# Flamingo block: transposed FFN tile in the down projection's bank, centred residual on ScalarE, quantisation factors on GpSimd, one addition of maxima divided over VectorE and ScalarE

## What is computed

```python
def _bitlinear(x, w):
    return jnp.einsum('bsi,oi->bso', _act_quant(x), _weight_quant(w))
# _act_quant: scale = 127 / max|x| per row; round(x * scale) / scale
# _weight_quant: scale = 1 / mean|w|; clip(round(w * scale), -1, 1) / scale

x = x + tanh(g_xattn) * attention(layernorm(x), ctx, ctx)      # softmax(q k / 4 + causal) v, then Wo
y = layernorm(x)
x = x + tanh(g_ffn) * bitlinear(silu(bitlinear(y, w_gate)) * bitlinear(y, w_up), w_down)
```

## Time and profile before

| | |
|---|---|
| median of 3 runs | 1917.84 us (1916.58 to 1918.06) |
| profiled execution | 1916.38 us |
| its span, first to last instruction | 1914.7 us |
| PE busy | 1618.2 us, 85% |
| DVE busy | 1568.8 us, 82% |
| ACT busy | 1193.0 us, 62% |
| POOL busy | 1130.4 us, 59% |
| mean granted TensorE clock | 0.986 of full speed |

### The profile page before, as it was taken

How to read it: one execution, slowest core, us unless ns; L and a number is a source line. 1 busy time by engine, 2 the same in 40 slices (tenths; PEclk the granted TensorE clock), 3 DMA queues, 4 the chain that set the end, 5 groups by cost and what they waited for, 6 DMA issues and landing times.

```text
span 1914.7 us, 45148 instructions
## 1 busy us (share of the span) xinstructions
PE 1618.2 (85%) x15430; PEld 1306.4 (68%) x15430; DVE 1568.8 (82%) x3481; ACT 1193.0 (62%) x2505; POOL 1130.4 (59%) x1745
## 2 busy tenths in 40 slices
PE   3688888888888888888888888888888888888874
PEld 2667767777776776777777776677677777677752
DVE  4388888888888888888888888888888888888884
ACT  2366666666666666666666666666666666666652
POOL 4556666656666566566665666656656666566621
PEclk9899999999999999999999999999999999999997
DMA  3322222222222322322222222232232222222200
GB/s 107 106 82 96 76 85 90 83 87 81 96 74 81 100 75 78 98 76 84 92 80 90 81 94 76 81 100 76 78 98 75 86 90 76 92 84 91 74 26 11
DMA packets 116595, 158.25 MB, mean 83 GB/s; under 512 B 14609, under 2 KB 66961, under 8 KB 116369
## 3 DMA queue, kind: packets, MB, share of 16 engines
q1 hardware_dynamic: 115088, 155.24, 24.6%
q10 hardware_dynamic: 1280, 0.14, 0.1%
HBM read 37.88 MB, written 16.78 MB: 29 GB/s over the span
## 4 chain that ended last, share of the span: by engine, by line
PE 48%; DVE 16%; issue 15%; ACT 15%; POOL 2%; POOLq 0%; ACTq 0%; DVEq 0%
PE psum L574 12%; PE psum L493 7%; PE psum L590 7%; ACT h_t L714 6%; PE psum L483 6%; PE psum L516 5%; PE psum L559 5%; DVE h L795 4%; DVE gu L791 4%; ACT prob_t L684 3%; PE psum L468 3%; DVE st L810 3%; DVE x L807 3%; PE psum L475 3%; ACT o_raw L720 2%
## 5 line engine op out<-in xcount | busy, mean ns | idle before, releaser
L768 DVE TENSOR_REDUCE row_max<-psum 128x8 f32<-128x1024 f32 x256 | 311.0, 1215 | 20.0 <-PE psum L475 19.5
L677 ACT ACTIVATE s_low<-psum,row_max 128x128 f32<-128x128 f32 x1024 | 279.6, 397 | 16.6 <-DVE row_max L768 16.5
L684 ACT ACTIVATE prob_t<-psum 128x1024 f32<-128x1024 f32 x256 | 262.3, 1025 | 32.0 <-PE psum L483 27.8
L483 PE MATMUL psum<-ident,s_low 128*128 128x128 f32 x2048 | 266.6, 274 | 0.2
L483 PEld LDWEIGHTS psum<-ident,s_low 128*128 128x128 f32 x2048 | 236.2, 142 | 24.9 <-DVE s_low L775 0.6
L971 POOL TENSOR_SCALAR hq<-h,sm 128x1024 f16<-128x1024 f32 x128 | 142.9, 1116 | 181.6 <-DVE sm L847 181.6
L791 DVE SCALAR_TENSOR_TENSOR gu<-th,psum 128x512 f32<-128x512 f32 x256 | 174.8, 683 | 84.3 <-ACT th L692 83.9
L692 ACT ACTIVATE th<-psum,sm 128x512 f32<-128x512 f32 x256 | 184.4, 720 | 80.5 <-PE psum L574 80.5
L951 POOL TENSOR_SCALAR xc<-x,ln 128x256 f32<-128x256 f32 x128 | 61.3, 479 | 282.9 <-DVE ln L816 282.9
L574 PE MATMUL psum<-wg_t,xq_t 128*128 128x512 f16 x512 | 154.9, 384 | 70.3 <-DVE h L795 70.3
L475 PE MATMUL psum<-k_stk,q_stk 128*128 128x256 f32 x1024 | 211.0, 328 | 0.0
(11 more groups left out here) (112 smaller groups left out, 3607.6 us busy)
## 6 DMA issues: line engine op xcount, KB each, us to landing
k_stk<-k_t SPq DMA_DIRECT2D x384, 128.0 KB, 2.3
q_stk<-q_t SPq DMA_DIRECT2D x192, 256.0 KB, 2.5
c_in<-in_ctx SPq DMA_DIRECT2D x64, 256.0 KB
x_in<-in_x SPq DMA_DIRECT2D x64, 256.0 KB
out<-y SPq DMA_DIRECT2D x128, 128.0 KB
g_nat<-in_L_ffn_w_gate SPq DMA_DIRECT2D x1, 1024.0 KB, 8.3
g_nat<-in_L_ffn_w_up SPq DMA_DIRECT2D x1, 1024.0 KB, 10.7
g_nat<-in_L_ffn_w_down SPq DMA_DIRECT2D x1, 1024.0 KB, 12.6
```

The lines of the kernel that those rows point to most:

```text
L483: last = nc.tensor.transpose(S_B[half][:, n * P:(n + 1) * P], s_low[:, HPC * half + n, :], ident[:, :])
L677: last = nc.scalar.activation(s_low[:, HPC + n, :], S_B[1][:, n * P:(n + 1) * P], ACT.Identity, bias=row_max[:, HPC + n:HPC + n + 1])
L684: nc.scalar.activation(prob_t[:, HPC * half:HPC * (half + 1), :].rearrange("p h k -> p (h k)"), S_B[half], ACT.Exp).then_inc(p_ok[half], 1)
L768: nc.vector.tensor_reduce(out=row_max[:, HPC * half:HPC * (half + 1)], in_=S_B[half].rearrange("p (h k) -> p h k", k=P), axis=AX.X, op=ALU ...
```

## The change

Six things are changed.

1. `T16`, into which `hidden_t` transposes hq, moves from bank 5 to bank 7. PE's `gate_up(0)` no longer waits for h_t of its section but for h of the section before; `hidden_t` takes over the waits for y, the residual and v_sb that `down` had.
2. xc is made by ACT (`centre`): x1 times -1 plus the mean. Its sign is the opposite of before, and the rounded gate and up matrices are made with a minus sign at set-up. The negated mean on DVE (L815) and xc on POOL (L951) go.
3. The factors L831 and L847 are made by POOL, ahead of the quantisation that uses them.
4. The addition of maxima for half 0 is divided: DVE does heads 0 to 3 with one instruction of 128x512, ACT does heads 4 to 7 with four of 128x128 (`shift_first`).
5. The order in the bodies of PE, DVE, ACT and POOL is another, and on ACT it differs between even and odd sections.
6. `values` comes with half 0 first.

```diff
-        T16 = bank(5).bitcast(F16)
+        T16 = bank(7).bitcast(F16)
...
                 def gate_up(c, half):
                     if half == 0:
                         pe.wait_ge(xqt_ok, c.tile(2))
-                        wait(pe, ht_ok, c.tile(3))
+                        wait(pe, h_ok[1], c.tile(3))
...
                 def hidden_t(c):
+                    wait(pe, y_ok, c.tile(4))
+                    pe.wait_ge(x1_ok, min(c.tile(2), N_SEQ))
+                    if c.s == 0 and c.spreads:
+                        pe.wait_ge(v_ok, c.even + 4)
                     pe.wait_ge(hq_ok, c.tile(3))
...
                 def shifted_t(c, half):
                     pe.wait_ge(s_sub[half], c.tile(0))
+                    if half == 0:
+                        pe.wait_ge(s_sub_act, c.tile(0))
...
+                def shift_first(c):
+                    act.wait_ge(s_max[0], c.tile(0))
+                    wait(act, p_tr[0], c.tile(1))
+                    for n in range(HPC // 2, HPC):
+                        last = nc.scalar.activation(s_low[:, n, :], S_B[0][:, n * P:(n + 1) * P], ACT.Identity,
+                                                    bias=row_max[:, n:n + 1])
+                    last.then_inc(s_sub_act, 1)
...
+                def centre(c):
+                    act.wait_ge(ln2_ag, c.tile(1))
+                    wait(act, xq_ok, c.tile(2))
+                    nc.scalar.activation(xc[:, :], x1[:, 1 - c.s, :], ACT.Identity, bias=mv2[:, 0:1], scale=-1.0).then_inc(xc_ok, 1)
...
-                    nc.vector.tensor_tensor(s_low[:, 0:HPC, :], S_B[0].rearrange("p (h k) -> p h k", k=P),
-                                            row_max[:, 0:HPC].unsqueeze(2).to_broadcast((P, HPC, P)), ALU.add).then_inc(s_sub[0], 1)
+                    few = HPC // 2
+                    nc.vector.tensor_tensor(s_low[:, 0:few, :], S_B[0][:, 0:few * P].rearrange("p (h k) -> p h k", k=P),
+                                            row_max[:, 0:few].unsqueeze(2).to_broadcast((P, few, P)), ALU.add).then_inc(s_sub[0], 1)
...
-                    nc.vector.tensor_scalar(ln2[:, 0:1], mv2[:, 0:1], -1.0, None, ALU.mult)
...
-                    dve.wait_ge(x_rcp_ok, c.tile(1))
-                    nc.vector.tensor_scalar(row(sm, t, X_FACTOR), row(sm, t, X_RCP), ln2[:, 2:3], QMAX,
-                                            ALU.mult, ALU.mult).then_inc(x_factor_ok, 1)
...
-                    dve.wait_ge(h_rcp_ok, c.tile(2))
-                    nc.vector.tensor_scalar(row(sm, t, H_FACTOR), row(sm, t, H_RCP), row(sm, t, H_OWN), QMAX,
-                                            ALU.mult, ALU.mult).then_inc(h_factor_ok, 1)
...
-                    nc.gpsimd.tensor_scalar(xc[:, :], x1[:, t, :], ln2[:, 0:1], 1.0, ALU.add, ALU.mult).then_inc(xc_ok, 1)
...
                 def quantise(c):
+                    pool.wait_ge(x_rcp_ok, c.tile(1))
+                    nc.gpsimd.tensor_scalar(row(sm, t, X_FACTOR), row(sm, t, X_RCP), ln2[:, 2:3], QMAX,
+                                            ALU.mult, ALU.mult).then_inc(x_factor_ok, 1)
...
                 def quantise_hidden(c):
+                    pool.wait_ge(h_rcp_ok, c.tile(2))
+                    nc.gpsimd.tensor_scalar(row(sm, c.s, H_FACTOR), row(sm, c.s, H_RCP), row(sm, c.s, H_OWN), QMAX,
+                                            ALU.mult, ALU.mult).then_inc(h_factor_ok, 1)
```

More of the change, by code:

```diff
@@ L184, in _ @@
                     act.wait_ge(g_rnd, n + 1)
-                    nc.scalar.activation(g_tern[:, n, :], g_nat[:, n, :], ACT.Copy, bias=-ROUND32).then_inc(tern, 1)
+                    sign = -1.0 if n < 2 else 1.0
+                    nc.scalar.activation(g_tern[:, n, :], g_nat[:, n, :], ACT.Copy, bias=-sign * ROUND32, scale=sign).then_inc(tern, 1)
             @block.gpsimd
@@ L630, in body @@
                         if c.attn:
+                            values(c, 0)
                             values(c, 1)
-                            values(c, 0)
                     else:
@@ L641, in body @@
                             inputs_t(c)
+                        if c.outp:
+                            out_natural(c)
+                        if c.ffn:
+                            gate_up(c, 0)
                         if c.down:
@@ L733, in body @@
                 def body(c):
[L734 to L755, removed]
-                    if c.attn:
-                        values(c)
+                    if c.s == 0:
+                        if c.ffn:
+                            quant_t(c)
+                        if c.attn:
+                            shift_first(c)
+                        if c.projects:
+                            inputs_t(c)
+                        if c.down:
+                            hidden_t(c)
+                        if c.outp:
+                            out_t(c)
+                        if c.ffn:
+                            tanh(c, 0)
+                        if c.attn:
+                            shift(c)
+                            exp(c, 0)
+                        if c.outp:
+                            centre(c)
+                        if c.ffn:
+                            tanh(c, 1)
+                        if c.projects:
+                            project_qk(c)
+                        if c.attn:
+                            exp(c, 1)
+                            values(c)
+                    else:
+                        if c.ffn:
+                            quant_t(c)
+                        if c.projects:
+                            inputs_t(c)
+                        if c.attn:
+                            shift_first(c)
+                        if c.ffn:
+                            tanh(c, 0)
+                        if c.down:
+                            hidden_t(c)
+                        if c.outp:
+                            out_t(c)
+                        if c.attn:
+                            shift(c)
+                        if c.ffn:
+                            tanh(c, 1)
+                        if c.attn:
+                            exp(c, 0)
+                        if c.projects:
+                            project_qk(c)
+                        if c.outp:
+                            centre(c)
+                        if c.attn:
+                            exp(c, 1)
+                        if c.projects:
+                            project_v(c)
+                        if c.attn:
+                            values(c)
@@ L767, in top @@
                     wait(dve, s_sub[half], c.tile(1))
+                    if half == 0:
+                        wait(dve, s_sub_act, c.tile(1))
                     nc.vector.tensor_reduce(out=row_max[:, HPC * half:HPC * (half + 1)],
@@ L812, in residual @@
                     wait(dve, ln2_rs, c.tile(2))
+                    wait(dve, xc_ok, c.tile(2))
                     nc.vector.bn_aggr(out=mv2[:, :], in_=st2[:, :]).then_inc(ln2_ag, 1)
                     dve.wait_ge(ln2_ag, c.tile(1))
-                    nc.vector.tensor_scalar(ln2[:, 0:1], mv2[:, 0:1], -1.0, None, ALU.mult)
                     nc.vector.tensor_scalar(ln2[:, 1:2], mv2[:, 1:2], LN_EPS, None, ALU.add).then_inc(ln2_sm, 1)
@@ L905, in body @@
                             top(c, 1)
+                        if c.norm:
+                            first_norm(c)
+                        if c.ffn:
+                            gated(c, 0)
                         if c.outp:
```

58 lines of the change are left out of this document (23 added, 35 removed).

## The result

The changed kernel takes 1726.76 us (median of 4 runs, 1725.98 to 1727.33), the kernel before 1917.93 (median of 4). The ratio is 0.900, with a 95% interval of 0.899 to 0.902: 191 us less, where 184 were forecast. The predicted time was 1734, the range 1698 to 1805.

What follows compares the result with a forecast made beforehand. No engine is full; a chain from engine to engine bounds the kernel. PE's 23.5 us a pair plus 1.6 of waits gives 25.1, taken as 25.3 against 28.31; over 61 pairs 184 us less, so 1734 us, range 1698 to 1805.

Steps and rivals of the forecast that it cites:

- The walk: Hand layout of a two-section pair, each step at the latest of engine, inputs and 0.05 us signal: 25.1 us.
- The allowance: 0.2 us a pair added to the walk's 25.1, giving 25.3.
- the jitter: Reason given for the 0.2: DVE and PE arrive within 0.2 us of each other at three places.
- The sum: 61 x (28.31 - 25.3) = 184 us off 1916.4 gives 1733; the runs' median is 1.5 higher, so 1734.
- Fill and drain left as they are: First 93 and last 95 us of the kernel taken as unchanged, between 8 us less and 8 more.
- the larger part: Claim that the new order of work on PE and DVE matters more than moving work; no separate size given.
- PE nearly full: Rival 1, chance 0.11: waits of 0.40, 0.38 and 0.4 close; a pair takes 24.4 us, the kernel 1678 us.
- ACT's queue as the chain: Rival 2, chance 0.19: half of ACT's added 3.0 us lands on the chain; 26.6 us a pair, 1813 us.
- xc behind q_f: Rival 3, chance 0.05: in odd sections, late xc delays the next maximum; at 3.5 us late, 28.6 a pair, 1936 us.

Runs made afterwards that it cites:

- order and bank alone: The changed kernel with whole addition and factors back on VectorE and centring back on GpSimd, order and bank 7 kept: 1826.4 us, 26.91 a pair (one run).
- the parts alone: Kernel before, its order and bank 5, plus divided addition, xc on ScalarE, factors on GpSimd, with ScalarE's additions behind h_t and o_t: 1909.8 us, ratio 0.996.
- bank 5: The changed kernel with T16 back in bank 5, down ahead of gate and up 0, h_t and o_t ahead of the first tanh in odd sections: 2038.9 us.

## Why the prediction was right

**The walk.** It was the part that carried the number, and step by step it holds. In the kernel after, even section from values (904.14) to values 11.83 us, 11.7 in the walk; odd section 13.57, 13.4. Gate and up 0 at 894.21 - 890.57 = 3.64 into the odd section, 3.4 in the walk, because the transposed inputs started at 2.21 and not at 2.1, and x_f's path took 1.43 from there, not 1.3; the wait is named 0.38, forecast 0.40. Down 6.36 into the section, 6.2 in the walk; half 1 at 7.24, 7.1. The waits for o_n, h and x_f are where the walk has them, and h_t's in the odd section, 0.30 us from start to start; its 0.1 in the even section is not there (down starts at 908.88, right behind gate and up). DVE's next maximum starts 0.62 after values in even sections and 1.63 after them in odd ones, 0.6 and 1.75 in the walk.

**The allowance.** The walk gave 25.1, I took 25.3, the chip has 25.41, so the 0.2 was of the right size, though not for the jitter that I gave as its reason: nearly every pair takes 25.40. In odd sections 0.17 is missing: the walk let the transposed inputs follow the scores and left out their wait for xq_t (2.21 after values; the kernel with xq_t first has the 2.04 of the walk's own steps), and the signal from ACT to PE ahead of gate and up 0 is 0.15 and not 0.05 (x_f ends at 894.06, PE starts at 894.21); the shorter wait for h_t gives a little of it back. In even sections 0.13 is missing, of which 0.1 is between scores and values (914.97 to 915.97, where the walk has 0.90). What holds it is not shown; k_f had ended at 915.14, 0.83 before values, and with the k projection moved, where it ends 1.49 before them, scores and values stand 1.00 apart as well (902.80 to 903.80).

**The sum.** Two terms were off. The steady part of 61 periods gave 61 x 2.90 = 177 us where 184 were forecast. "Fill and drain left as they are (between 8 less and 8 more)" was mis-sized: of the 190 us by which the span shrank they gave the other 13. The two misses have opposite signs and partly cancel, which is luck: the span is 1724.8 against 1731. That the part behind the last copy shrank by 11.6 us was read from the two spans; why was not tested.

**The parts.** DVE busy 22.17 a pair (22.1 forecast), ACT 20.96 (21.5 forecast: the new records sum to 3.3 us a pair, but overlap their neighbours, so that its busy time grew by 2.5), POOL 17.65. That order is "the larger part" is wrong as it stands: order and bank alone give 91 us, the parts alone 8, and both together 191. Order is a condition for the rest, and I did not see that 92 of the 191 us come only from both together. In forecasting the two halves I was wrong about the parts in the old order by 24 us beyond my range (1928.9 against 1880 to 1905), and about the order alone by 11.

**The rivals.** PE nearly full, 24.2 to 24.9 a pair, did not happen: the waits stayed, and even with the k projection moved forward a pair takes 25.06. ACT's queue as the chain happened neither; the kernel with eight heads on ACT shows where it would begin. The Trainium skill, ScalarE: Activation LUTs, Rules for kernel authors, would keep additions on VectorE. The trace agrees with the cost (1.15 us on ACT for 0.53 on DVE), and the times disagree with the rule here: following it for the additions of maxima costs 14 us against the change, and going the whole way against it 105. xc behind q_f cost nothing that shows.

## What to carry to other kernels

When no engine is full, lay out one period by hand from the trace, with each step at the latest of its engine and its inputs: it gave the period here within 0.3 us of 25.4, while busy shares (PE 85%, DVE 82%) point at DVE's load, whose relief alone was worth 8 of the 191 us. Moving load off an engine that is not in the loop is worth little until the loop is shortened, and then it may be worth as much as shortening the loop was (100 and 91 us here); so test such edits together as well as one by one. When moving work to an idle engine, look at what stands behind it in that engine's list, and divide it where the whole is too long.

## What the runs showed of the hardware

Where TensorE had one wait of 2.72 us in every pair (h behind the residual), or of 2.22 with others of 0.84, 0.65 and 0.33 beside it (bank 5), it cost more than its own length. In the kernel with h behind the residual, PE is busy 0.90 of 3.60 us ahead of the fall, and the granted clock is 0.72 and 0.75 in the two stretches behind it (columns as in the windows above):

```profile
689.00:692.60 3.60, 0.90 (x8) 0.70 (x6) 2.53 (x8) 2.58 (x7) 0.66 (x2) 1.00 0.83 263
692.60:695.70 3.10, 3.08 (x17) 2.71 (x18) 2.31 (x9) 0.69 (x1) 2.26 (x5) 0.72 0.00 0
695.70:699.00 3.30, 3.30 (x39) 2.97 (x42) 2.24 (x5) 1.86 (x3) 2.08 (x5) 0.75 0.00 0
```

Means between half and full, that is, part of the stretch at 1.2 GHz and part at 2.4. It happens in 20 and 49 of the 60 pairs and not in the others, which have the same wait, and adds 1.5 to 1.6 us each time (29.44 against 27.85, 30.58 against 29.06). The Trainium skill, TensorE: Matmul & The Clock Gate, Part 1: The HAM clock gate, says that the clock is slow by default and released by activity. The trace agrees: the clock fell behind a stretch with little work on PE, and it is 1.00 again from 699.00 on, behind 6.40 us in which PE was busy 6.38. Neither the kernel before nor the one after has such a fall in its steady part, where the granted clock is 1.00 in all 60 pairs. Why only some pairs fall is open.
